# An attention and nearest-neighbour kernel: stage A in equal slots of gather units, squared norms as three bf16 rows, coordinate table by DMA

## What is computed

```
def _chunk_attn(q, k, v, masks, W_in, b_in, W_out, b_out):
    scores = jnp.einsum('bnqhd,bnkhd->bnhqk', qh, kh) * scale
    scores = scores + jnp.where(km[:, :, None, None, :] > 0, 0.0, NEG)
    attn = jax.nn.softmax(scores, axis=-1)
...
def _knn(p, k):
    xx = jnp.sum(p * p, axis=1)
    pd = 2.0 * jnp.einsum('bdn,bdm->bnm', p, p) - xx[:, :, None] - xx[:, None, :]
    return jax.lax.top_k(pd, k)[1]
...
    idx = _knn(x_loc, k)
    pts = x_loc.transpose(0, 2, 1)
    rel = pts[bidx, idx] - pts[:, :, None, :]
```

## Time and profile before

| | us |
|---|---|
| median of 3 runs | 6767.1 (6765.2 to 6777.43) |
| profiled execution | 6742.75, span 6740.7 |
| TensorE, VectorE busy | 5081.5, 5407.4 |
| ScalarE, GpSimd busy | 4017.7, 2186.1 |

### The profile page before, as it was taken

The page is one execution under the profiler, slowest core; times in us unless marked ns, Lnnn a source line. Parts: engine busy times, 40 slices in busy tenths (PEclk is TensorE's granted clock), DMA queues, the critical chain, the costliest instruction groups (busy, mean ns, idle before and its releaser), DMA issues. The chain is left out here.

```text
span 6740.7 us, 167741 instructions
## 1 busy us (share of the span) xinstructions
PE 5081.5 (75%) x63700; PEld 2978.5 (44%) x64334; DVE 5407.4 (80%) x7613; ACT 4017.7 (60%) x9098; POOL 2186.1 (32%) x2884
## 2 busy tenths in 40 slices
PE   6777777777777777777777777777105779999999
PEld 3444444444444444444444444444102356666666
DVE  8887777778777877878777787876479998888887
ACT  4666666666665665666566666666434367667676
POOL 2454444445444444544444454444100000000000
PEclk8778787878878787887878788787557889999999
DMA  0000000000000000000000000000000000000000
GB/s 33 19 14 14 14 14 14 23 17 14 14 14 14 14 20 21 14 14 14 14 14 24 17 14 14 14 14 11 1 0 0 0 21 33 28 28 29 28 28 28
DMA packets 35800, 114.08 MB, mean 17 GB/s; under 512 B 5488, under 2 KB 6128, under 8 KB 34800
## 3 DMA queue, kind: packets, MB, share of 16 engines
q1 hardware_dynamic: 34928, 102.28, 4.2%
HBM read 68.71 MB, written 33.55 MB: 15 GB/s over the span
## 5 line engine op out<-in xcount | busy, mean ns | idle before, releaser
L449 PE MATMUL g_ps<-tparts,ohT 128*128 128x24 bf16 x23040 | 921.4, 178 | 936.2 <-ACT ohT L551 897.0
L551 ACT ACTIVATE ohT<-oh_ps,cst 128x512 bf16<-128x512 f32 x1920 | 1279.7, 692 | 389.4 <-PE oh_ps L431 199.2
L449 PEld LDWEIGHTS g_ps<-tparts,ohT 128*128 128x128 bf16 x23040 | 765.6, 100 | 1442.0 <-ACT ohT L551 1339.4
L795 DVE MAX8 vals<-pd_sb 128x8 f32<-128x1024 f32 x1024 | 1205.4, 1213 | 133.6 <-ACT pd_sb L551 112.7
L800 DVE FIND_INDEX8 idx<-vals,pd_sb 128x8 uint16<-128x1024 f32 x1024 | 1244.1, 1218 | 0.0
L802 DVE MATCH_REPLACE8 pd_sb<-vals,pd_sb 128x1024 f32<-128x1024 f32 x768 | 927.6, 1208 | 0.0
L551 ACT ACTIVATE pd_sb<-pd_ps,nxx 128x512 f32<-128x512 f32 x512 | 355.3, 694 | 856.5 <-PE pd_ps L355 854.8
L1849 PEld LDWEIGHTS e_a_ps<-planes,e_oh 120*128 120x128 bf16 x24576 | 688.7, 98 | 265.3 <-issue 182.3
L819 DVE TENSOR_REDUCE mx<-s_ps 128x8 f32<-128x512 f32 x256 | 176.5, 689 | 714.5 <-PE s_ps L390 714.5
L1620 ACT COPY e_at<-e_a_ps 128x512 f32<-128x512 f32 x512 | 542.9, 1060 | 341.2 <-PE e_a_ps L1849 336.0
L1849 PE MATMUL e_a_ps<-planes,e_oh 120*128 120x32 bf16 x24576 | 701.6, 178 | 46.9 <-DVE e_oh L1777 46.9
(11 more groups left out here) (225 smaller groups left out, 7194.4 us busy)
## 6 DMA issues: line engine op xcount, KB each, us to landing
ctx_s<-in_ctx SPq DMA_DIRECT2D x32, 512.0 KB, 4.2
maskb<-in_mask_Bx1x_ff SPq DMA_DIRECT2D x32, 512.0 KB, 5.0
x_s<-in_x SPq DMA_DIRECT2D x32, 512.0 KB, 5.7
y_spill<-y_s SPq DMA_DIRECT2D x32, 512.0 KB, 2.9
e_y<-y_spill SPq DMA_DIRECT2D x32, 512.0 KB, 3.9
out<-e_o SPq DMA_DIRECT2D x64, 256.0 KB, 2.0
pd_sb<-in_shape_constants SPq DMA_DIRECT2D x1, 1024.0 KB, 4.9
cst<-in_shape_constants SPq DMA_DIRECT2D x1, 242.5 KB, 2.6
```

What stands on the lines that cost most here:

```text
L449: m = nc.tensor.matmul(g_ps[:, k % GK, t, :], ohT[:, k % 2, bass.ts(t, P)], tparts[:, par, part, :], start=(part == 0), stop=(part == PART ...
L551: return nc.scalar.activation(dst, src, func, scale=scale, bias=bias)
L795: nc.vector.max(vals[:, i, :], pd_sb[:, (t + i) % RING, :]).then_inc(topk_step, 1)
```

## The change

It touches stage A alone.

- Every slot now has two distance halves, of the tile two ahead, and eight or seven gather units (`unit_starts` 0, 7, 15, 22, 30), laid out alike: unit, half, unit, half, unit, scores, unit, transposes, unit, values, unit, the rest, two units.
- Fills stand two units ahead, `ohT` has three buffers, and `g_ps` two banks; `pd_ps` gives one of its two away. The bias of the one-hot is now the eighth row of the code, so ScalarE's ReLU has none, and `bitsb` keeps ones there.
- The squared norms: `squares` multiplies -0.5 by `sq` once a batch, ScalarE moves the result to rows 0, 64 and 96 of `xp` in bf16 and to `xs`, and GpSimd subtracts and casts in four steps (`squares_split`, slot 4), so that three bf16 rows add up to the fp32 norm. Distances and norms multiply by `ones3` in bf16. The inverted mask `minv` now sits in rows 32 to 63 of `xp` and is made by GpSimd.
- `table` comes by three DMAs from `ctx` instead of `coordinates`; they stand in SyncE's queue behind the loads of x and mask, and behind the end of the gathers of two batches ago.
- `digits` writes both outputs so that the innermost elements are contiguous. `vz` has one half, and `project_values` moves to slots 0 and 4.

```
-        unit_starts = (0, 4, 15, 21)
+        unit_starts = (0, 7, 15, 22, 30)
...
+            def load_table(b, par):
+                places = table[:, par, :].rearrange("p (t c) -> p t c", c=3)
+                for c in range(3):
+                    sp.dma_start(places[:, :, c], ctx[b][c].rearrange("(t p) -> p t", p=P),
+                                 allow_slow_non_contiguous=True).then_inc(table_landed[par], 16)
...
-                if not (isinstance(n, int) and n < 2):
-                    pe.wait_ge(pd_moved, n - 1)
-                nc.tensor.matmul(pd_ps[:, h, :], ctx_s[:, par, bass.ts(t, P)], ctx_s[:, par, bass.ts(h, HALF)],
+                if not (isinstance(n, int) and n < 1):
+                    pe.wait_ge(pd_moved, n)
+                if t == 0 and h == 0:
+                    pe.wait_ge(xp_ready, b + 1)
+                nc.tensor.matmul(pd_ps[:], ctx_s[:, par, bass.ts(t, P)], ctx_s[:, par, bass.ts(h, HALF)],
                                  start=True, stop=False)
-                nc.tensor.matmul(pd_ps[:, h, :], neghalf[:], sq[:, bass.ts(h, HALF)],
+                nc.tensor.matmul(pd_ps[:], ones3[0:XR, :], xp[0:XR, par, bass.ts(h, HALF)],
                                  start=False, stop=True).then_inc(pd_ready, 1)
...
+                    if k + 2 < K:
+                        fill(b, q, k + 2)
+                    if k % GK == 0 and not (isinstance(gg, int) and gg < 2):
+                        pe.wait_ge(g_moved, gg - 1)
...
+            def squares(mv_, b, par):
+
+                if not (isinstance(b, int) and b == 0):
+                    act.wait_ge(xp_ready, b)
+                for h in range(2):
+                    ps = mv_.next()
+                    move(xp[0:32, par, bass.ts(h, HALF)], ps[0:32]).then_inc(xx_moved, 1)
+                    move(xp[64:P, par, bass.ts(h, HALF)], ps[64:P]).then_inc(xx_moved, 1)
+                    move(xs[64:P, bass.ts(h, HALF)], ps[64:P]).then_inc(misc_moved, 1)
...
-                nc.vector.tensor_tensor(bits16[:].rearrange("p t k e -> p (t k) e"),
-                                        flat.rearrange("p (m o) -> p m o", o=1).to_broadcast([P, m, BITS]),
-                                        bitval[:].rearrange("p (o e) -> p o e", o=1).to_broadcast([P, m, BITS]),
+                picked = idx16[:, par, q * QT:(q + 1) * QT]
+                m = QT * 2
+                nc.vector.tensor_tensor(bits16[:],
+                                        picked.rearrange("p t (h o k) -> p (t h) o k", h=2, o=1).to_broadcast([P, m, BITS - 1, KT]),
+                                        bitval[:].rearrange("p (o e) k -> p o e k", o=1).to_broadcast([P, m, BITS - 1, KT]),
                                         ALU.bitwise_and).then_inc(bits_ready, 1)
...
+            def squares_split(b, par, moved):
+
+                gate(pool, minv_ready, b + 1, pool_gates)
+                gate(pool, misc_moved, moved, pool_gates)
+                pool.wait_ge(xx_moved, (b + 1) * 4)
+                nc.gpsimd.tensor_tensor(xs[64:P, :], xs[64:P, :], xp[64:P, par, :], ALU.subtract).then_inc(xp_step, 1)
+                gate(pool, xp_step, b * 3 + 1, pool_gates)
+                nc.gpsimd.tensor_copy(xp[64:P, par, :], xs[64:P, :]).then_inc(xp_step, 1)
+                pool.wait_ge(xp_step, b * 3 + 2)
+                nc.gpsimd.tensor_tensor(xs[96:P, :], xs[96:P, :], xp[96:P, par, :], ALU.subtract).then_inc(xp_step, 1)
+                gate(pool, xp_step, b * 3 + 3, pool_gates)
+                nc.gpsimd.tensor_copy(xp[96:P, par, :], xs[96:P, :]).then_inc(xp_ready, 1)
```

More of the change, by code:

```diff
@@ new lines, in emit @@
+                    if quarter == 0 and not first:
+                        turned = turn_bits(misc, b - 1, h)
+                    unit()
+                    ahead(0)
+                    unit()
+                    ahead(1)
+                    unit()
+                    if quarter < QT - 1:
+                        scores(b, par, t + 1)
+                    elif ongoing:
+                        scores(nb, npar, (t + 1) % TILES)
+                    unit()
+                    if before:
+                        probs_in = turn_probs(misc, b if t > 0 else b - 1, (t - 1) % TILES)
@@ new lines, in emit @@
+                    unit()
+                    if before:
+                        moved = values(misc, (t - 1) % TILES, probs_in)
+                    unit()
+                    if quarter == 0 and before:
+                        rows(misc, moved)
+                    if quarter == 0:
+                        project_values(misc, par, h)
+                    if quarter == 2 and ongoing:
+                        queries_keys(misc, npar, nh)
+                    if t == 3 and not last:
+                        squares(misc, b + 1)
@@ L527, in rows @@
+                    if t == 5 and not last:
+                        norms(misc, b + 1, 1 - par)
+                    unit()
+                    unit()
             def rows(misc, moved):
@@ new lines, in emit @@
+                    unit()
+                    ahead(1)
+                    unit()
+                    unit()
+                    if before:
+                        turned_probs(mv_)
+                    unit()
+                    if before:
+                        values(mv_, (t - 1) % TILES)
+                    unit()
+                    if quarter == 0 and before:
+                        rows(mv_, b if t > 0 else b - 1, 0 if t > 0 else 1)
+                    if quarter == 0:
+                        project_values(mv_)
@@ L686, in exponents @@
+                    if quarter == 2 and ongoing:
+                        queries_keys(mv_, nb, nh)
+                    if t == 3 and not last:
+                        squares(mv_, b + 1, 1 - par)
+                    if t == 5 and not last:
+                        normed = norms(mv_, 1 - par)
+                    unit()
+                    unit()
             def exponents(s, t):
```

357 lines of the change are left out of this document (156 added, 201 removed).

## The result

The changed kernel takes **6510.6 us** (median of 4 runs, 6502.9 to 6511.1) against 6768.3 for the kernel before (4 runs): ratio 0.961, 95% interval 0.960 to 0.963. It is 258 us faster; the forecast was 597 us faster, and the result lies 50 us above the end of the range. The sign was right, the size was not. Its profiled execution spans 6501.1 us at a mean granted clock of 0.866 (0.812 before).

The account below looks back on a forecast made before the run. It took TensorE and ScalarE in lockstep as the bound, then a loop through GpSimd's `kz`: 12.3 + 25.3 + 3.8 + 21.6 = 63.0 us a half, 128.5 a batch with 2%, hence 6170 us; range 5930 to 6460.

Parts of the forecast that it names:

- What bound the kernel before: Steady stage A: TensorE and ScalarE in lockstep carry the batch; VectorE gets scores late, idling 23.6 us a batch there.
- TensorE's products: Distances and norms in bf16: TensorE needs about 13 us a batch less at a clock of 0.80.
- Gather units: Fills two ahead, three `ohT` buffers, two `g_ps` banks: TensorE's 28.2 us a batch of waits mostly go.
- VectorE, GpSimd, DMA: VectorE's work falls from 116.5 to about 113.4 us a batch; GpSimd's added 5 to 9.5 us is covered; table loads cost nothing.
- the late table: Rival, chance 0.05: table DMAs land late, GpSimd stands at the split in slot 3; at 56 us, 6980 us.
- What is late next: Slots 3 and 7: GpSimd waits for `digits` before two gathers, so `kz` comes 12.4 us after the maximum and sets the period.
- the loop: Path per half batch from maximum through `kz`, scores and exponents to the next odd maximum: 63.0 us, 126 a batch.
- the predicted wait: TensorE waits at the scores for GpSimd's `kz`, 3 to 8 us long, in slots 3 and 7 only.
- the 2%: Allowance because the same adding on the kernel before gave 36.0 us against 36.8 measured: 126 becomes 128.5 us a batch.
- The clock takes it back: Rival: all at half clock, 141 us a batch, 6560 us; chance 0.23 together with "it doesn't do what it says".
- VectorE alone: Rival, chance 0.12: VectorE the only bound, 113.4 to 116 us a batch, if GpSimd's gathers ran earlier; 5770 us.
- it doesn't do what it says: Rival: two-ahead fills gain nothing, only products shrink, 10 us a batch, 6460 us; chance 0.23 together with the clock rival.

Follow-up runs that it names:

- Keys first with the zero product: keys first plus a third fp32 product, of a zero tile with the contexts, in each distance half: 5999.0 us.
- Three gsb: The changed kernel with a third buffer for copied gather groups (`gsb`), GpSimd's order kept: 6504.3 us, 139.9 us a batch.
- keys first: The changed kernel with GpSimd, in slots 2 and 6, doing gather groups, then key spreading for slots 4 and 0, then `convert`: 5831.3 us.
- the wait filled and `squares` earlier: Three gsb with `squares` moved from slot 3 to slot 2 and 40 overwritten bf16 products ahead of TensorE's wait for `kz`: 6233.9 us.
- groups first: The changed kernel with GpSimd doing its two gather groups before the conversion of the bits in slots 2 and 6: 6080.8 us.
- digits early: The changed kernel with VectorE's `digits` after round 0 instead of round 2 in slots 2 and 6: 6158.3 us.

## Why the prediction missed

**What bound the kernel before: right.** Reordering GpSimd there moves nothing, and the wait for scores went (23.6 to 0.5 us a batch) when TensorE's and ScalarE's slots shrank.

**TensorE's products: about right.** TensorE is busy 103.4 us a batch (2217.66 / 21.44), 10.2 less than the earlier trace rows where 13 was forecast. The comparison is rough: part of the 10.2 is the clock (0.87 against 0.80), and the trace of before lacks a third of the fills (813 records of 1219). Keys first with the zero product shows that about half of such time counts where VectorE is near its bound.

**Gather units: the mechanism right, its worth too high.** Waits of TensorE for `ohT` fell from 28.2 to about 1 us a batch (16.9 us ahead of the fills and at most 2.1 ahead of the products, in 21.44 batches). Undoing the edit brings back 16 to 17 us of waits but only 6.9 and 8.9 us of time.

**VectorE, GpSimd, DMA: right.** `bits` takes 615 ns (0.60 forecast), `hi1h` 658 (0.64), a batch 113.0 us of work (113.4). GpSimd's inversion and four split steps take 9.1 us (5 to 9.5 forecast), and no engine waits for them in the loop. The table's loads land in a median of 5.8 us (96 of them), so the late table was no danger, and GpSimd never waits there.

**What is late next: this step failed, in two ways.** First, the loop was entered at the wrong instruction. The prediction saw that GpSimd waits for `digits` with work behind it, but followed only `kz`. The two gather groups stand in the same queue, and the two-buffered `gsb` ties ScalarE to the first of them. The prediction's own reading of the earlier trace rows names the groups. ScalarE's copy of group 3 comes before the scores (2027.68 and 2037.31 in the timeline of the changed kernel), so it stood first; it covered the wait for `kz`, which in the changed kernel hardly shows (one wait of 2.8 us in the whole run). Three gsb shows that this alone changed no time: with the buffer free, the predicted wait appears in the predicted slots and the period is the same 139.9. "I am wrong if TensorE does not wait for `kz`" was therefore true of the row and not of the cause, which is GpSimd's place at `convert`.

Second, the size. The predicted wait was to be 3 to 8 us; in three gsb it is 10 to 12, because TensorE reaches these scores about 1 us after the maximum and not 4. The loop was to be 63.0 us a half, 126 a batch and 128.5 with the 2%; it is 139.9. Three gsb has the predicted path, so its timeline shows which term is off. There the mean half of 1000 to 4000 us is:

| from | to | sum, us | three gsb, us |
|---|---|---|---|
| maximum of slots 2 and 6 | scores of slots 3 and 7 | 12.3 | 12.4 |
| those scores | scores of slots 4 and 0 | 13.7 | 20.9 |
| those | scores of slots 5 and 1 | 14.6 | 14.2 |
| those | maximum of slots 6 and 2 | 22.4 | 22.5 |

The mis-sized term is the second one, where the sum had (6.1 + 3.5 + 2.6) x 1.12, the 2.6 being the exponents ahead of the later scores. It is 7 us a half short and makes up all of the 13.9 us between 126 and 139.9. Three things are known of it. `squares`, which the sum spread over all slots as 0.4 us each, lies in it once a batch and is worth 4.5 us a batch. A wait of 4 us ahead of the turned bits occurs once in two batches, for which the profile names no cause and which the kernel before has as well: the stretch from slot 7 to 0 takes 17.5 and 23.1 us in turn, 2.8 us a batch. And the clock behind the stand costs 4.9 us a batch; but that is no part of the miss, since the sum had allowed for it (128.5 at a clock of 0.80 against 122.6 at 1.0), only spread over all slots alike.

With the wait filled and `squares` earlier the clock is 0.96 and the period 131.5, to be set against the 122.6 of the sum at full clock. Some 9 us a batch therefore stay open; the wait of 4 us holds about 2.4 of them. They lie in the same stretch (16.3 us a half, where the sum had 12.2 at full clock) and in the slot behind it, whose agreement above is luck. These slots run at full clock in three gsb too, where the sum had 13.0:

```profile
2055.07:2069.33 14.26, 12.80 (x156) 7.32 (x158) 6.65 (x9) 10.74 (x34) 12.82 (x14) 1.00 0.01 2
```

The prediction called this slot ScalarE's, 12.5 us. ScalarE is busy 10.7 of 14.3 us in it and TensorE 12.8, so by the busy times the slot is TensorE's rather than ScalarE's; no run changes that slot alone, so this part stays argued.

**The rivals.** *The clock takes it back* gave 6560 and 141 us a batch, nearest in number, but by luck: the mean clock rose to 0.87, and the clock is low mainly in the stands and behind them. *VectorE alone* (5770) is where the kernel goes once its stated condition holds, gathers earlier on GpSimd: 5831 with keys first, where 113.6 us of the 117.8 are VectorE's work. *The table late* and *it doesn't do what it says* were not seen.

## What to carry to other kernels

When a wait is expected to surface on a queue, list everything that stands behind the waiting instruction, each with who wants it and through which buffer, and take the one that is wanted first; freeing that one alone can give nothing. Put an instruction that waits for the slowest engine last in its queue: here 430 and then 250 us for moving lines, with no work saved. In a sum of slots, put work that occurs once a batch into the slot where it lies, and price each slot on both engines at full clock. When a total agrees, compare its terms: here two totals agreed by luck (groups first, and the clock rival).

## What the runs showed of the hardware

- VectorE's short 16-bit operations nearly double or worse beside GpSimd's: `hi`, 295 ns while GpSimd stands still, takes 1996 ns in the mean with digits early. In the timeline it starts 0.45 us after GpSimd's `kz` and ends 0.17 us after it. The Trainium skill, "SBUF — State Buffer", section "Who interferes with whom", says that VectorE in a two-port mode and GpSimd share a pair of ports, which the one that issues first holds for its whole instruction while the other is blocked; the row of `hi` agrees, though no row shows its mode. It also says that a VectorE instruction with two inputs in SBUF contends with a GpSimd instruction that reads SBUF; `bits` (1136 ns against 615) and `hi1h` (1259 against 658) agree. GpSimd's stand at `convert` had so far kept the digits fast.
- Keeping TensorE busy with useless products during a wait that it could not avoid was worth 165 us (143 with `squares` earlier). Behind the wait the granted clock was then 1.00 over 23 us and not 0.71.
- Loads of 4 KB in runs of four bytes landed in 5.8 us, hardly later than the 512 KB loads (4.8 us for `ctx_s`).
